# Layernorm of the next chunk between the products of the present one, in the projections and in the expert phase

## What is computed

```python
def _layernorm(x, eps=1e-5):
    return (x - mean(x)) / sqrt(var(x) + eps)
# block 1: 8 rounds of relu(a + shift(up) @ W2.T + b2), both directions, mixed by W3, W4
h = _L0_tok_ref(x, ...)
# block 2, on x = _layernorm(h), 8 heads of 64:
v = x @ wqv_w.T + wqv_b                  # q, vf, vb: 3 x 512 numbers a token
k = x[:, :, None, :] * wk
a = softmax(-sum(|q - k|) / sqrt(64))    # L1 distance, with one extra zero row
o = sum over heads of (a.T @ vf + a @ vb)
h = h + x + (o * sigmoid(1.702 * o)) @ fanin_w.T + fanin_b
# block 3, on x = _layernorm(h): two of 8 experts
combine = softmax over the top 2 of (x @ Wg.T + bg)
for e in range(8):
    out += combine[e] * (relu(x @ W1[e].T + b1[e]) @ W2[e].T + b2[e])
h = h + out
```

## Time and profile before

| what | value |
|---|---|
| median of 3 runs | 8705.82 us (8699.16 to 8708.18) |
| the profiled execution | 8702.39 us, span 8700.6 us, granted clock 0.992 |
| PE busy | 8578.6 us (99%) |
| ACT, DVE, POOL busy | 7719.9, 7229.9, 56.3 us |
| DMA | 114.26 MB, mean 13 GB/s |
| attention stage | 267.2 to 8393.6 us of the span |

### The profile page before, as it was taken

The page is one execution under the profiler, slowest core; times in us unless marked ns, Lnnn a source line. Parts: engine busy times, 40 slices in busy tenths (PEclk is TensorE's granted clock), DMA queues, the critical chain, the costliest instruction groups (busy, mean ns, idle before and its releaser), DMA issues. The chain is left out here.

```text
span 8700.6 us, 248840 instructions
## 1 busy us (share of the span) xinstructions
PE 8578.6 (99%) x111814; PEld 6465.3 (74%) x111814; DVE 7229.9 (83%) x5624; ACT 7719.9 (89%) x3709; POOL 56.3 (1%) x39
## 2 busy tenths in 40 slices
PE   8899999999999999999999999999999999999989
PEld 3488997989756875778946897478966687688973
DVE  4788888888888888888888888888888888888862
ACT  3799999999999999999999999999999999999965
POOL 1000000000000000000000000000000000000000
PEclk9999999999999999999999999999999999999989
DMA  4200000000000000000000000000000000000000
GB/s 140 68 17 2 17 2 17 2 2 17 2 17 2 17 2 2 17 2 17 2 17 2 5 14 2 17 2 17 2 6 13 2 17 2 17 2 2 2 12 8
DMA packets 135375, 114.26 MB, mean 13 GB/s; under 512 B 111464, under 2 KB 114984, under 8 KB 134040
## 3 DMA queue, kind: packets, MB, share of 16 engines
q1 hardware_dynamic: 121611, 78.49, 3.9%
q10 hardware_dynamic: 12692, 19.51, 0.7%
HBM read 57.74 MB, written 40.22 MB: 11 GB/s over the span
## 5 line engine op out<-in xcount | busy, mean ns | idle before, releaser
L781 PE MATMUL sc<-ring,window 128*32 128x375 f32 x96000 | 7894.0, 479 | 19.7 <-DVE ring L900 16.7
L832 ACT ACTIVATE ring<-qx,xs 128x3000 f32<-128x3000 f32 x2624 | 7176.4, 2791 | 622.4 <-PE sc L781 619.4
L781 PEld LDWEIGHTS sc<-ring,window 128*32 128x32 f32 x96000 | 5792.5, 110 | 1752.3 <-issue 539.6
L900 DVE TENSOR_SCALAR ring<-qx,xs 128x3000 f32<-128x3000 f32 x3376 | 6130.5, 1836 | 1049.8 <-PE sc L781 991.3
L850 DVE COPY sc<-kept 128x750 f32<-128x750 f32 x385 | 361.6, 939 | 76.8 <-ACT ex L817 53.5
L748 PEld LDWEIGHTS acc<-ext,vf 128*32 128x32 f32 x9408 | 374.0, 109 | 42.6 <-issue 12.6
L735 PE MATMUL acc<-ex,vb 128*32 128x375 f32 x3088 | 398.5, 477 | 1.5 <-DVE ex L865 1.5
L748 PE MATMUL acc<-ext,vf 128*32 128x128 f32 (+1 forms) x9408 | 387.6, 270 | 0.2 <-DVE ext L876 0.2
L876 DVE STREAM_TRANSPOSE ext<-ex 128x768 f32<-128x768 f32 x385 | 374.1, 972 | 0.6
L817 ACT ACTIVATE ex<-sc 128x750 f32<-128x750 f32 x385 | 298.1, 774 | 5.6 <-PE sc L781 5.6
L735 PEld LDWEIGHTS acc<-ex,vb 128*32 128x32 f32 x3088 | 203.0, 108 | 57.3 <-issue 16.6
(11 more groups left out here) (173 smaller groups left out, 896.8 us busy)
## 6 DMA issues: line engine op xcount, KB each, us to landing
qx<-scratch_qk SPq DMA_DIRECT2D x60, 375.0 KB
scratch_v<-ext SPq DMA_DIRECT2D x21, 960.0 KB, 9.7
scratch_qk<-qx ACTq DMA_DIRECT2D x32, 375.0 KB, 8.0
vb<-scratch_v SPq DMA_DIRECT2D x120, 92.0 KB
vf<-scratch_v SPq DMA_DIRECT2D x120, 88.0 KB
scratch_v<-ext ACTq DMA_DIRECT2D x4, 960.0 KB, 10.6
xs<-scratch_x SPq DMA_DIRECT2D x15, 187.5 KB
vb<-scratch_v SPq DMA_DIRECT2D x120, 1.8 KB
```

Of the source, the lines that this page charges most:

```text
L781: mm = pe.matmul(bank[32 * j:32 * j + 32, h, 0:HALF], window[:, HALF_NH * g + j, ROWS - 1 - i:3 * ROWS - 1 - i], ring[:, slot, j, h * HALF ...
L832: act.activation(flat(ring[:, (HALF * g + k) % RING, :, :]), flat(qx[g][:, :, :]), ACT.Abs, bias=xs[g][:, 1, k:k + 1], scale=0.5).then_inc ...
L900: vec.tensor_scalar(flat(ring[:, (HALF * g + k) % RING, :, :]), flat(qx[g][:, :, :]), xs[g][:, 0, k:k + 1], xs[g][:, 1, k:k + 1], ALU.max, ...
```

## The change

It has three parts.

1. In `phase_tokens` only chunk 0 is normalized ahead of the projections, with its mean ahead of the sign products. Then `q` and `v` of chunk c alternate with the steps of the layernorm of the next chunks, one step (`mean`, `var`, `spread` on PE, with their partners on ACT and DVE) after each sequence or v chunk, and then with the six ksum products. For their banks q gives up its second PSUM buffer. SP stores `scratch_x` after v chunk 13 and the parts of ksum after v chunks 16, 18 and 19 (before: first of all, and after 8, 10 and 12). POOL adds `hx` after the splitting, not ahead of it.
2. ACT issues the first pair's loads right after the last q, ahead of the steps and v stores that are left.
3. `phase_feed` is cut the same way: chunk 0 goes through fan, layernorm, gates and shares alone, and those of chunk c + 1 stand between the experts of chunk c, at fixed places. The loop has one expert a step. The products up are fp32 (four a step), and the bf16 parts of `xt` and of the expert weights are gone. Gating works on one chunk (64 elements), six times, with an Exp and a Sqrt each. The gate products take both halves in one product. POOL keeps only two memsets, two small copies and the cast of `pick`.

The diff, cut to its core:

```diff
-            pq = [psum(inner, f"pq{k}", [128, 2, 512]) for k in range(2)]
+            pq = psum(inner, "pq", [128, 2, 512])
             pv = [psum(inner, f"pv{k}", [128, 2, 512]) for k in range(2)]
+            px = psum(inner, "px", [128, 512])
+            py = psum(inner, "py", [128, 512])
...
+            NSTEP = 3 * (NQC - 1)
...
+                    def step(u):
+                        if u < NSTEP:
+                            (mean, var, spread)[u % 3](1 + u // 3)
+                        elif u < NSTEP + NQC:
+                            sums(u - NSTEP)
...
                         for p in range(HP):
                             n = b * HP + p
-                            if n >= 2:
-                                pe.wait_ge(q_made, n - 1)
+                            if n:
+                                pe.wait_ge(q_made, n)
...
+                    u = 0
                     for c in range(NQC):
+                        for b in batches_of(c):
+                            q(b)
+                            step(u)
+                            u += 1
+                        for k in chunks_of(c):
+                            v(k)
+                            step(u)
+                            u += 1
...
+                        for b in batches_of(c):
+                            q(b)
+                            step(u)
+                            u += 1
+                            if b == B - 1:
+                                first_pair()
+                        for k in chunks_of(c):
+                            step(u)
+                            u += 1
+                            if k and on_act(k - 1):
+                                store_v(k - 1)
...
+        NI = NQC * NE
+        FAN_AT, MEAN_AT, VAR_AT, SPREAD_AT, GATE_AT, SHARE_AT, TURN_AT = 0, 1, 2, 3, 4, 6, 1
...
+                def ups(n):
+                    c, e = n // NE, n % NE
+                    pe.wait_ge(x_made, c + 1)
+                    for u in range(2):
+                        if n:
+                            pe.wait_ge(relu_made, 2 * n - 1 + u)
+                        m = (2 * e + u) * 128
+                        for h in range(2):
+                            mm = pe.matmul(pu[u][:, h, 0:EC], w1t[64 * h:64 * h + 64, m:m + 128],
+                                           xt[64 * h:64 * h + 64, cols(c)], start=True, stop=True)
+                        mm.then_inc(up, 1)
...
+                def downs(n):
+                    e = n % NE
+                    pe.wait_ge(relu_made, 2 * n + 2)
+                    if n:
+                        pe.wait_ge(c_used, n)
...
+                for n in range(NI):
+                    c, e = n // NE, n % NE
+                    if n + 1 < NI:
+                        relu(n + 1)
+                    keep(n)
+                    if e == TURN_AT and c:
+                        emit(c - 1)
+                    if c + 1 < NQC:
+                        if e == MEAN_AT:
+                            square(c + 1)
+                        if e == VAR_AT:
+                            root(c + 1)
+                        if e == GATE_AT:
+                            exps(c + 1)
+                        if e == SHARE_AT:
+                            first(c + 1)
+                            second(c + 1)
```

More of the change, by code:

```diff
@@ L499, in _ @@
                                        start=(p == 0), stop=(p == HP - 1))
                     mm.then_inc(signed, 1)
[L501 to L509 removed]
+                    var(0)
@@ L564, in root, with sums, step @@
                         act.wait_ge(var_sum, c + 1)
-                        act.activation(std[:, SUB * c:SUB * c + SUB, :], var_bank(c), ACT.Sqrt, bias=eps[0:CH, :]).then_inc(std_made, 1)
-                    def store_v(b):
-                        for c in chunks(b):
-                            if on_act(c):
-                                act.wait_ge(v_made, 2 * c + 2)
-                                act.dma_start(rows_v[c], vs[c % NVS]).then_inc(v_stored[c % NVS], 16)
-                    def store(n):
-                        act.wait_ge(q_made, n + 1)
-                        act.dma_start(scratch_qk[n, :, :], qs[n % NQS]).then_inc(q_stored[n % NQS], 16)
+                        act.activation(std[:, SUB * c:SUB * c + SUB, :], py[0:CH, 0:2 * SUB].rearrange("p (k a) -> p k a", a=2),
+                                       ACT.Sqrt, bias=eps[0:CH, :]).then_inc(std_made, 1)
+                    def sums(c):
+                        act.wait_ge(ks_sum, c + 1)
+                        act.activation(ks32[:, cols(c)], bank(c)[0:2 * NH, 0:EC], ACT.Identity, bias=bqs[:, :]).then_inc(ks_kept, 1)
+                    def step(u):
+                        if u < NSTEP and u % 3 == 0:
+                            square(1 + u // 3)
+                        if u < NSTEP and u % 3 == 1:
+                            root(1 + u // 3)
+                        if NSTEP <= u < NSTEP + NQC:
+                            sums(u - NSTEP)
                     def q(b):
@@ L595, in _ @@
+                    act.copy(wqs[64:128, 1, :], pq[64:128, 0, 0:NH]).then_inc(signed_kept, 1)
                     act.wait_ge(eps_set, 3)
-                    for c in range(NQC + 2):
-                        if c < NQC:
-                            square(c)
-                        if 0 <= c - 2 < NQC:
-                            root(c - 2)
-                    act.wait_ge(signed_kept, 2)
-                    q(0)
-                    for c in range(NQC):
-                        act.wait_ge(ks_sum, c + 1)
-                        act.activation(ks32[:, cols(c)], ks_bank(c), ACT.Identity, bias=bqs[:, :]).then_inc(ks_kept, 1)
@@ new lines, in phase_feed @@
+        cb = [sbuf(ctx, f"cb{k}", [128, EC]) for k in range(2)]
+        part = [sbuf(ctx, f"part{k}", [128, EC]) for k in range(2)]
+        acc = [sbuf(ctx, f"sum{k}", [128, EC]) for k in range(2)]
+        res = [sbuf(ctx, f"res{k}", [CH, SUB, 2, D]) for k in range(2)]
+        pu = [psum(ctx, f"pu{k}", [128, 2, 512]) for k in range(2)]
+        pd = psum(ctx, "pd", [128, 512])
+        pc = psum(ctx, "pc", [128, 512])
+        px = psum(ctx, "px_d", [128, 512])
+        py = psum(ctx, "py_d", [128, 512])
@@ new lines, in phase_feed @@
+        c_kept = semaphore(ctx, "c_kept")
+        down = semaphore(ctx, "down")
+        c_used = semaphore(ctx, "c_used")
+        y_added = semaphore(ctx, "y_added")
+        y_turned = semaphore(ctx, "y_turned")
+        y_kept = semaphore(ctx, "y_kept")
+        res_out = [semaphore(ctx, f"res_out{k}") for k in range(2)]
+        view = out.rearrange("b (h k p) d -> b k p h d", h=2, k=HALF // CH)
+        NI = NQC * NE
+        FAN_AT, MEAN_AT, VAR_AT, SPREAD_AT, GATE_AT, SHARE_AT, TURN_AT = 0, 1, 2, 3, 4, 6, 1
@@ new lines, in _ @@
+                gated(0)
+                vec.wait_ge(w_first, 48)
+                added(0)
+                center(0)
+                for c in range(1, NQC):
+                    gated(c)
+                invert(0)
+                normal(0)
+                vec.wait_ge(w_gate, 64)
+                choose(0)
+                vec.wait_ge(c_zero, 1)
+                left(0)
+                third(0)
+                vec.wait_ge(w_down, 48)
+                for n in range(NI):
+                    c, e = n // NE, n % NE
+                    add(n)
+                    if c + 1 < NQC:
+                        if e == FAN_AT:
+                            added(c + 1)
+                        if e == MEAN_AT:
+                            center(c + 1)
+                        if e == VAR_AT:
+                            invert(c + 1)
+                        if e == SPREAD_AT:
+                            normal(c + 1)
+                        if e == GATE_AT:
+                            choose(c + 1)
+                        if e == SHARE_AT:
+                            left(c + 1)
+                            third(c + 1)
```

879 lines of the change are left out of this document (379 added, 500 removed).

## The result

| | before | changed |
|---|---|---|
| median | 8705.82 us | 8666.46 us (8664.93 to 8670.50, 5 runs) |
| profiled execution | 8702.39 us | 8668.67 us, span 8666.9 us, clock 0.992 |
| ratio to before | | 0.9957, 95% interval 0.9942 to 0.9971 |

The account below looks back on a forecast made before the run. DMA stores were taken to bound the projections, a chain of small steps the feed front, PE the expert loop. Projections -10 and feed -48.4 made -58.4 from 8705.8: 8647 us, range 8628 to 8668.

Parts of the forecast that it names:

- The start of q: Projections: with only chunk 0 normalized ahead and its mean first, q starts 12.3 us earlier.
- One product costs about 1.9 us: Projections, single q buffer: 0.98 us ACT pass, 0.75 us product and two handovers; 32 products make 61 us.
- A v chunk leaves PE 0.7 us free: Projections: DVE needs 2.55 us a v chunk, PE 1.9, so only about 7 us of interleaved steps show.
- Production and DMA are nearly tied: Projections: supply takes 128 us, 295 GB/s against DMA's 286; 4 to 5 us taken off the gain.
- Rival (a): Projections: production bounds them, q buffer and steps eat the head start; gain 0 to 3 us, 8655, chance 0.15.
- my signs of being wrong: Loop clock under 0.9; ACT's loop waits over 30 us; projections ending before 250 or after 265.
- The order of the first pair's loads costs and brings nothing: End of projections: bytes in front of the end are the same in both versions, so 0 us.
- The front of the feed phase: One chunk's chain instead of six: first down product at 8422 instead of 8476.22, 54 us earlier.
- The expert loop: From the first down product on: 207 PE work + 12.5 stalls + 7.5 end = 227 us, before 224.4; 3 more for clock.
- the 2.5 us stalls at the Exp: Expert loop, fifth expert of a chunk: PE waits for ReLUs behind ACT's Exp, 2.5 us a chunk, 12.5 in all.
- The price of a table switch: Feed phase: 1.28 us a load, no drain; the skill's 2.66 us would mean some 10 us less gain, 8657.
- Rival (d): Expert loop: PE's clock falls to 1.2 GHz, up to about 8854; slower than before from 28% on; chance 0.03.

Follow-up runs that it names:

- e3: The kernel before with one q PSUM buffer instead of two, each product waiting for ACT's pass over the last: 8709.44 us, ratio 1.0009.
- e7: The changed kernel with TensorE's part of every layernorm step of chunks 1 to 5 issued twice: 8678.70 us, ratio 0.9971.
- e2: The kernel before with only the new `phase_tokens`, feed phase left old: 8719.35 us, ratio 1.0017.
- e5: The changed kernel with the first pair's loads moved behind all v chunks, to the end of ACT's list: 8671.57 us, ratio 0.9965.
- e8: The kernel before with fp32 products up, without the bf16 splits of x and w1, in its old order: 8678.65 us, ratio 0.9970.
- e11: The changed kernel with every q product issued twice into the same buffer with the same values: 8687.13 us, ratio 0.9981.
- e1: The kernel before with only the new feed phase, `phase_tokens` left old: 8649.55 us, ratio 0.9937.
- e12: Old projections with the new feed phase, the first pair's last 16 loads issued on SyncE's queue instead of ScalarE's: 8646.41 us, ratio 0.9938.
- e6: Old projections with the new feed phase, the first pair's loads issued in three parts behind the last three batches' q groups: 8644.33 us, ratio 0.9933.

## Why the prediction was wrong, point by point

- **The start of q.** Forecast 12.3 us earlier, measured 118.10 - 110.19 = 7.9. 2.6 us of it is this execution's later start. Of the 1.8 us that are left, 1.0 is the table load: it did not lie beside chunk 0's variance but behind the wait for it (105.53 - 2.6 = 102.9, where I had 101.9).
- **"One product costs about 1.9 us."** This step failed. It took 2.04 us at the upper clock and 2.70 to 2.76 at the lower. The 0.75 us came from a mean of overlapping instructions of a kernel with two buffers, and the clock in the new order was left out: the hand-off alone, in the old order, costs 62 us (e3), in the new order q costs 73 instead of 61.
- **"A v chunk leaves PE 0.7 us free", so 7 us of steps show.** This failed most: 26 us of steps stand in PE's line where I had 7. v chunk and step take 2.9 us, 1.9 + 1.0, against DVE's 2.55, and steps behind q groups have no cover at all. Doubling the layernorm steps (e7) adds 17 us of work and costs 12.2, so most of such work is on the path.
- **"Production and DMA are nearly tied."** Forecast 128 us, measured 165; the DMA share fell to 0.70. Measured apart: one buffer 5 us (e3, with an interval that reaches zero), the rest of the change 10 (e2 less e3), against a forecast gain of 10; since that rest holds the earlier loads, worth 5 (e5), the order itself cost more, some 15. Rival (a) had the mechanism, but its price stopped at a gain of 0 to 3: I did not let the new order lose, though PE's own sum would have shown it. How the order's cost divides between steps, clock and the later last q is not taken apart. Of my signs of being wrong, the third came: the last v chunk is added at 275.2, outside 250 to 265.
- **"The order of the first pair's loads costs and brings nothing."** Wrong by 5 us (e5), in the change's favour. In the runs in which the loads go out in one piece, attention starts 25 to 35 us after the first of them. They stand behind the last q, and the new order has that at 257 instead of 235, with two q groups in a row behind which DVE stands 17.8 us.
- **The front of the feed phase.** Right: 26.7 against 28.1 us, gating steps 0.22 to 0.23 us as worked out. That the order by chunks makes it was right too (e8).
- **The expert loop.** The sum was right by luck: 226.9 measured, 227 forecast and 3 more for a low clock at its start, which didn't come (1.00). An expert costs 4.03 us, not 3.72 (up 1.88 for 1.70, down 1.83 for 1.75, share 0.32 for 0.265): 48 times 0.31 is 15 us more. The steps of a chunk cost PE 5.2 to 5.4 us, not 5.8: 3 less. And the 2.5 us stalls at the Exp, 12.5 us, don't exist. I had counted load and Exp behind DVE's steps; the load lay ahead of them (1.28 us), the shift was ready at 3.2 us instead of 3.45, and PE came for the ReLU at 4.9 instead of 4.4. The first ReLU was done at 4.5. By these rows a load behind the wait would have cost less than 1 us a chunk, an estimate from the times above, so most of the stall was mis-sized even with the load where I had it. "fp32 products up thus only pay for the interleaved work" held: 20 us gained, 23 put in.
- **The price of a table switch.** The Trainium skill (ScalarE: Activation LUTs, What ACT_TABLE_LOAD costs) would have made five switches cost more; in the loop they lie in the wait and cost nothing on the path, and the next activation begins 0.01 us after a load of 1.28 (8452.10, 8453.39), so the drain that it adds does not show. Its estimate, 8657, is closer than mine to 8666, but not by its reason.
- **The clock.** Rival (d) did not come in the loop (granted 1.00), but it came in the projections, where I hadn't looked for it: 0.78 in the new stretch.

## What to carry to other kernels

When an engine that was not the bottleneck gets work between its products, write out its own line end to end, waits for hand-offs included, and compare it with the stretch; a small slack per piece is used up by the first step put into it. Interleave where a chain of small steps kept a full engine idle (the feed phase: 44 us off the front, 23 into the loop; the rest of its 55 us is the arithmetic) and leave it where another resource had the stretch filled (the projections, +15 us): test the two halves of such a change apart. Put loads that wait for nothing ahead, but count each issue against the engine whose queue it stands in, at the price it has while the DMA engines are full.

## What the runs showed of the hardware

- An ACT table load (1.28 us) can run ahead of the semaphore wait of its activation: load at 8461.51, the Exp itself waiting until 8465.04, five times in the loop. At 105.53 here and at 8456.91 before it stood behind the wait.
- Where PE waits 1.1 us for each product, the same product takes 1.62 us or 0.90, at granted levels of 1.2 and 2.4 GHz. With its work doubled and the same waits (e11) 18 instead of 11 of the 32 ran at the upper level.
- Code that is the same as before had a granted clock of 0.87 in one execution's layernorm and 0.50 in another's (e8).
- Sixteen DMA issues took 6.2 us on ScalarE at the end of e1, most of them 0.32 to 0.34 each, and 15.0 on SyncE in e12, beside ScalarE's. Ten took 14.8 us on ScalarE in e6 at a DMA share of 0.95.
- Eight fp32 instructions of 500 columns over 64 rows take 1.88 us in the changed loop, 0.18 more than 1.70, which I had by taking the last one's tail off.
